# A recommendation model on one core: rows and dense inputs from dumped halves, and two of the first layer's three parts as split float32r passes

## The reference

```
emb = tables[field, sparse]                       # (2048, 26, 32)
linear = lin_sparse_w[field, sparse].sum(-1) + dense @ lin_dense_w
for (w, b) in ((conv1_w, conv1_b), (conv2_w, conv2_b)):     # x0 = xk = emb
    hp = einsum('bhd,bmd->bhmd', xk, x0)          # all products of rows
    xn = sigmoid(w @ hp + b)                      # 128 rows x 32
    xk, rest = xn[:, :64], xn[:, 64:];  keep rest
cin  = concat(rests).sum(-1) @ cin_w + cin_b
deep = tanh chain 845 -> 1024 -> 512 -> 256 on [emb, dense], then @ deep_w + deep_b
out  = linear + cin + deep + bias
```

## Time and profile before

| | before |
|---|---|
| runs, us | 1644.03, 1645.74, 1645.41 (median 1645.41) |
| profiled execution, us | 1642.12, its span 1640.3 |
| PE busy | 1566.3 us, 95% |
| DVE busy | 1143.2 us, 70% |
| ACT busy | 704.7 us, 43% |
| POOL busy | 763.8 us, 47% |
| DMA | 277.60 MB, mean 169 GB/s |
| granted TensorE clock, mean | 0.995 |
| the 64 steps | about 66 to 1354 us |
| the deep layers | 1362 to 1630 us |

### The profile page before, as it was taken

One profiled execution on the slowest core, in us unless ns is written; L12 is line 12 of the kernel. 1 busy time (PEld: TensorE's weight loads), 2 busy tenths in 40 slices (PEclk: granted clock), 3 DMA queues, 4 the chain that ended last, 5 costly groups with the idle time before them and its releaser, 6 DMA issues.

```text
span 1640.3 us, 23407 instructions
## 1 busy us (share of the span) xinstructions
PE 1566.3 (95%) x6840; PEld 681.2 (42%) x6840; DVE 1143.2 (70%) x992; ACT 704.7 (43%) x981; POOL 763.8 (47%) x631
## 2 busy tenths in 40 slices
PE   0599999999999999999999999999999997999998
PEld 0233333333333333333333333333333336787876
DVE  3287878787878787878787878787878783434432
ACT  1344444343444444444344444343444424444543
POOL 7657474757474656565655655664742010000000
PEclk9999999999999999999999999999999999999999
DMA  4688787888887888888888888888888762232231
GB/s 93 124 195 199 189 198 192 194 193 191 196 194 194 194 194 190 193 188 193 195 194 194 194 191 192 193 195 193 196 194 193 185 150 92 92 101 86 89 107 39
DMA packets 111803, 277.60 MB, mean 169 GB/s; under 512 B 26036, under 2 KB 46804, under 8 KB 111704
## 3 DMA queue, kind: packets, MB, share of 16 engines
q1 hardware_dynamic: 98456, 270.11, 66.0%
q0 software_dynamic: 13312, 7.06, 5.3%
HBM read 270.03 MB, written 7.04 MB: 169 GB/s over the span
## 4 chain that ended last, share of the span: by engine, by line
PE 94%; POOL 2%; DVE 1%; ACT 1%; issue 1%; DMA 0%; ACTq 0%; DVEq 0%; POOLq 0%
PE y L636 45%; PE xn L630 21%; PE bc L750 16%; PE bc L616 5%; PE bc L623 3%; PE bc L599 2%; POOL emb L443 2%; PE bc L608 1%; DVE xb L554 0%; ACT sq L806 0%; DVE hp L554 0%; DVE x_lo L563 0%; PE xn L767 0%; DMA sum<-sparse 0%; DMA emb<-table,idx_stage 0%
## 5 line engine op out<-in xcount | busy, mean ns | idle before, releaser
L554 DVE TENSOR_TENSOR hp<-bc,xk 128x1024 f32<-128x1024 f32 x384 | 448.9, 1219 | 264.2 <-PE bc L616 264.2
L554 DVE TENSOR_TENSOR xb<-xb,xk 128x1024 f32<-128x1024 f32 x448 | 581.4, 1355 | 22.8 <-ACT xk L811 22.8
L443 POOL DMA_INDIRECT emb<-table,idx_stage x416 | 495.8, 1192 | 145.9 <-issue 130.5
L636 PE MATMUL y<-xb,w2s 128*64 128x512 f32 x1792 | 423.6, 599 | 0.3 <-ACT r L816 0.3
L636 PE MATMUL y<-hp,w2s 128*64 128x512 f32 x1536 | 368.2, 600 | 0.0
L630 PE MATMUL xn<-sq,w1s 128*128 128x512 f32 x768 | 363.0, 609 | 5.4 <-ACT sq L806 3.2
L806 ACT ACTIVATE sq<-bc 128x1024 f32<-128x1024 f32 x192 | 182.9, 1027 | 261.3 <-PE bc L623 261.3
L810 ACT ACTIVATE xk<-xn,bias 64x512 f32<-64x512 f32 x128 | 87.3, 682 | 376.4 <-PE xn L630 376.4
L458 POOL TENSOR_TENSOR r<-r 128x512 f32<-128x512 f32 x96 | 148.7, 1549 | 144.1 <-ACT r L816 98.4
L630 PEld LDWEIGHTS xn<-sq,w1s 128*128 128x128 f32 x768 | 136.6, 191 | 183.3 <-issue 157.1
L636 PEld LDWEIGHTS y<-xb,w2s 128*64 128x64 f32 x1792 | 117.2, 136 | 214.6 <-issue 188.3
(11 more groups left out here) (63 smaller groups left out, 1056.4 us busy)
## 6 DMA issues: line engine op xcount, KB each, us to landing
xb<-x_rows SPq DMA_DIRECT2D x896, 256.0 KB, 4.9
w_raw<-W SPq DMA_DIRECT2D x32, 448.0 KB, 3.3
w_raw<-W SPq DMA_DIRECT2D x16, 512.0 KB, 3.3
emb<-table,idx_stage POOLq DMA_INDIRECT x416
x_rows<-deep_t SPq DMA_DIRECT2D x16, 384.0 KB
w_raw<-W SPq DMA_DIRECT2D x8, 256.0 KB, 2.7
hp<-select SPq DMA_DIRECT2D x2, 512.0 KB, 4.8
x_rows<-deep_t SPq DMA_DIRECT2D x16, 45.0 KB
```

The costliest lines, as they stand in the source:

```text
L443: nc.gpsimd.indirect_dma_start(out=emb[:, m, :], out_offset=None, in_=table, in_offset=bass.IndirectOffsetOnAxis(ap=idx_stage[:, m:m + 1], ...
L554: nc.vector.tensor_tensor(product(n)[:, :], x[:, :], xk[sl % 2][:, :], ALU.mult).then_inc(multiplied, 1)
L636: last = nc.tensor.matmul(y2[H * c:H * c + H, :], w2s[:, ORDER[n], :], src[:, c * CHUNK:(c + 1) * CHUNK], start=(n == 0), stop=(n == PAIRS ...
```

## The change

- `turn_x0`, `make_high` and `make_low` go. ScalarE's `turned_deep` copies each of now three D fills twice, to `deep_t` (one tile now) and rounded to `deep_halves`; VectorE's `lower_deep` makes the rest; SP dumps both halves to `x0_halves` in HBM and loads `x0t` from there (`load_rows`, four DMAs a step). The D fills stand in step 1 and ahead of fills 3 and 4.
- Of the first layer's three parts, two (k < SPLIT = 2) are made as float32r passes: ScalarE squares them twice (float32 and rounded), GpSimd makes the rest of part 0 and VectorE that of part 1 (`lower_squares` on either engine), and `contract_k` makes three float32r matmuls for each; the third part stays float32. A step's rests are made ahead of contract_k(0) of the same step, which waits for them (`sq_lowered`).
- The deep layers' x is loaded from `x0_halves` and, for the dense inputs, from `dense_halves`, both split before; `upper_x` and `lower_x` go. Weights 0 and 1 are loaded at the start.
- BY_PE is 3, 4, 6, 7, 9, 10 instead of 3, 4, 7, 8, 9, 10; fills and contractions have another order; product 10 shares its buffer with product 3. A spread pair is three DMAs (64, 32 and 32 partitions) instead of two, of the same bytes. GpSimd's order changes. `r1` and `r2` keep a running total in slot 3. Some of the output's terms are moved into the last step, and the four output rows are one instruction.

```
-ORDER = [3, 10, 4, 0, 7, 11, 5, 1, 8, 2, 9, 12, 6]
-BY_PE = (3, 4, 7, 8, 9, 10)
+PER_GROUP = 16
+
+
+ORDER = [0, 1, 2, 3, 8, 4, 5, 9, 6, 7, 10, 11, 12]
+BY_PE = (3, 4, 6, 7, 9, 10)
 assert sorted(ORDER) == list(range(PAIRS))
 BY_DMA = tuple(n for n in range(PAIRS) if n not in BY_PE)
 
 
 
 
-
 STEP_WORK = (
     ("fill", (("K", 0), ("K", 1), ("K", 2))),
-    ("of_last", (9, 10, 11, 12)),
-    ("fill", (("T", 0), ("D", 0), ("D", 1))),
+    ("of_last", (6, 7, 8, 9, 10, 11, 12)),
+    ("fill", (("D", 0), ("D", 1), ("D", 2))),
+    ("fill", (3, 4)),
     ("first", 0),
-    ("fill", (3, 4)),
-    ("of_this", (0, 1, 2)),
+    ("fill", (6, 7)),
+    ("of_this", (0, 1, 2, 3)),
+    ("fill", (9, 10)),
     ("first", 1),
-    ("fill", (7, 8)),
-    ("of_this", (3, 4)),
-    ("fill", (9, 10)),
-    ("of_this", (5, 6, 7, 8)),
+    ("of_this", (4, 5)),
 )
 LEFT = STEP_WORK[1][1]
-SL_DEEP = 2
-DEEP_PARTS = range(0, 4), range(4, KD)
+SL_DEEP = 1
+DEEP_PARTS = range(0, 3), range(3, 5), range(5, KD)
 SLOTS = 3
+R_SLOT = 0, 1, 2, 1
...
+            def dump_halves(t):
+                sp.wait_ge(deep_lowered, t * 2 + 2)
+                hold()
+                for i in range(2):
+                    sp.dma_start(x0_halves[bass.ds(t, 1), i, 0:(KD - 1) * P, :].rearrange("t (k p) b -> p (t k) b", p=P),
+                                 deep_halves[:, i, 0:KD - 1, :].bitcast(F32)).then_inc(halves_dumped, 16)
+                    sp.dma_start(x0_halves[bass.ds(t, 1), i, (KD - 1) * P:M * ROW, :].rearrange("t p b -> p (t b)"),
+                                 deep_halves[0:LAST_E, i, KD - 1, :].bitcast(F32)).then_inc(halves_dumped, 16)
+
+            def await_halves(t):
+                sp.wait_ge(halves_dumped, t * (32 * DUMPS) + 32 * DUMPS)
+                hold()
+
+
+            def load_rows(t, sl):
+                for half in range(2):
+                    rows = x0_halves[bass.ds(t, 1), half, :, :].rearrange("t (m e) b -> (t m) e b", e=ROW)
+                    for c in range(2):
+                        first = sl * STEP_D + c * Q
+                        start = H * c + half
+                        sp.dma_start(x0t[sl][start:start + 2 * M:2, :].bitcast(F32),
+                                     rows[:, first:first + Q, :].rearrange("m d b -> m (d b)")).then_inc(x0_loaded[sl % 2], 16)
+
+
+            def load_x(g, part, parts):
+                loads = []
+                for i, x in enumerate((x_hi, x_lo)):
+                    for k in range(KD):
+                        rows = P if k < KD - 1 else LAST_E
+                        src = x0_halves[bass.ds(g * (CHUNK // P), CHUNK // P), i, k * P:k * P + rows, :]
+                        loads.append((x[0:rows, k, :].bitcast(F32).rearrange("p (t b) -> p t b", b=P),
+                                      src.rearrange("t p b -> p t b")))
+                    loads.append((x[LAST_E:LAST_K, KD - 1, :].bitcast(F32), dense_halves[i, :, bass.ds(g * CHUNK, CHUNK)]))
+                for dst, src in loads[part * X_LOADS // parts:(part + 1) * X_LOADS // parts]:
+                    sp.dma_start(dst, src).then_inc(x_loaded, 16)
...
+                for f, parts in PAIR_ROWS:
                     first = (2 * ORDER[BY_DMA[i]] + f) * ROW + sl * STEP_D
                     row = x0_rows[bass.ds(t, 1), first:first + STEP_D, :].rearrange("t d b -> t (d b)")
-                    sp.dma_start(xb[i][H * f:H * f + H, :], row.to_broadcast([H, COLS])).then_inc(spread[i], 16)
+                    sp.dma_start(xb[i][parts, :], row.to_broadcast([parts.stop - parts.start, COLS])).then_inc(spread[i], 16)
...
+                        if i == 2 and sl == SL_DEEP + 1 and ahead > 0:
+                            dump_halves(t + 1)
+                        if i == 3 and sl == SL_DEEP + 1 and ahead > 0:
+                            await_halves(t + 1)
+                        if i == 3 and (sl < 2 or ahead > 0):
+                            if is_first and sl == 0:
+                                sp.wait_ge(filled, PRO_FILLS)
+                            load_rows(t + (sl + 2) // STEPS, (sl + 2) % STEPS)
+                    if sl == SL_DEEP and ahead > 0:
+                        dump(t + 1)
+                    if sl == 2 and ahead == 0:
+                        sp.wait_ge(dense_dumped, 64)
+                        load_x(0, 0, 1)
...
+            def lower_squares(s):
+                pool.wait_ge(squared, squared_by(s, 0))
+                nc.gpsimd.tensor_tensor(sq_lo[0][:, :], sq[0][:, :], sq_hi[0][:, :], ALU.subtract).then_inc(sq_lowered[0], 1)
...
+            lower_squares(-1)
+            free_emb(0, DEEP_N)
             gather(range(AHEAD[2]))
 
             def tile(t, is_first, ahead):
+                s = t * STEPS
+                lower_squares(s)
+                if ahead > 0:
+                    gather(range(AHEAD[2], M))
                 if not is_first:
                     add_up(t - 1, STEPS - 1, r2, r2_step, y2_read, 1, sum2)
+                lower_squares(s + 1)
+                add_up(t, 1, r1, r1_step, xn_read, 2, sum1)
+                if ahead > 1:
+                    free_emb(t + 1, filled_by(t, SL_DEEP, ("D", DEEP_N - 1), ahead))
+                    gather(range(AHEAD[0]))
+                lower_squares(s + 2)
+                add_up(t, 2, r1, r1_step, xn_read, 2, sum1)
+                if ahead > 1:
+                    gather(range(AHEAD[0], AHEAD[1]))
+                add_up(t, 1, r2, r2_step, y2_read, 1, sum2)
                 if ahead > 0:
-                    gather(range(AHEAD[2], M))
-                add_up(t, 1, r1, r1_step, xn_read, 2, sum1)
-                if ahead > 0:
-                    make_low(t + 1)
-                add_up(t, 2, r1, r1_step, xn_read, 2, sum1)
-                add_up(t, 1, r2, r2_step, y2_read, 1, sum2)
-                if ahead > 1:
-                    free_emb(t + 1, filled_by(t, SL_DEEP, ("D", 1), ahead))
-                    gather(range(AHEAD[0]))
+                    lower_squares(s + 3)
                 add_up(t, 3, r1, r1_step, xn_read, 2, sum1)
                 if ahead > 1:
-                    gather(range(AHEAD[0], AHEAD[1]))
+                    gather(range(AHEAD[1], AHEAD[2]))
                 add_up(t, 2, r2, r2_step, y2_read, 1, sum2)
-                if ahead > 1:
-                    gather(range(AHEAD[1], AHEAD[2]))
 
...
+            def lower_deep(t):
+                dve.wait_ge(deep_rounded, t * DEEP_N + DEEP_N)
+                for rows, ks in ((slice(0, P), slice(0, KD - 1)), (slice(0, LAST_E), slice(KD - 1, KD))):
+                    nc.vector.tensor_tensor(deep_halves[rows, 1, ks, :], deep_t[rows, ks, :],
+                                            deep_halves[rows, 0, ks, :], ALU.subtract).then_inc(deep_lowered, 1)
...
+            def lower_squares(s):
+                dve.wait_ge(squared, squared_by(s, 1))
+                nc.vector.tensor_tensor(sq_lo[1][:, :], sq[1][:, :], sq_hi[1][:, :], ALU.subtract).then_inc(sq_lowered[1], 1)
...
+                        if n == 2 and not (ahead == 0 and sl == STEPS - 1):
+                            lower_squares(s)
                         if n in BY_PE:
                             dve.wait_ge(filled, filled_by(t, sl, n, ahead))
-                            if not start:
-                                dve.wait_ge(contracted, contracted_by(s - 1, n))
+                            if n == BY_PE[-1]:
+                                dve.wait_ge(contracted, contracted_by(s, BY_PE[0]))
+                            elif not start:
+                                dve.wait_ge(contracted, contracted_by(s - 1, BY_PE[-1] if n == BY_PE[0] else n))
                             x = bc[slot_of(sl, n, ahead)]
                         else:
                             i = BY_DMA.index(n)
-                            dve.wait_ge(spread[i], s * 32 + 32)
+                            dve.wait_ge(spread[i], s * (16 * len(PAIR_ROWS)) + 16 * len(PAIR_ROWS))
                             x = xb[i]
                         nc.vector.tensor_tensor(product(n)[:, :], x[:, :], xk[sl % 2][:, :], ALU.mult).then_inc(multiplied, 1)
-                        if n == 8 and sl == 1 and ahead > 0:
+                        if n == 3 and sl == SL_DEEP and ahead > 0:
                             sum_linear(t + 1)
+                        if n == 7 and sl == SL_DEEP and ahead > 0:
+                            dve.wait_ge(halves_dumped, t * (32 * DUMPS) + 32 * DUMPS)
+                            lower_deep(t + 1)
...
-                for k in range(K1):
-                    last = nc.tensor.matmul(xn[:, :], w1s[:, k, :], sq[k][:, cols], start=(k == 0), stop=(k == K1 - 1))
+                for k in range(SPLIT):
+                    for i, (w, x) in enumerate(((w1_hi, sq_hi[k][:, cols]), (w1_lo, sq_hi[k][:, cols]),
+                                                (w1_hi, sq_lo[k][:, cols]))):
+                        nc.tensor.matmul(xn[:, :], w[:, k, :], x, start=(k == 0 and i == 0), stop=False)
```

(33 more changed lines are left out.)

354 lines of the change are left out of this document (171 added, 183 removed).

## The result

| | before | after |
|---|---|---|
| median, us | 1645.58 | 1703.41 (1699.85 to 1708.88, four runs) |
| ratio, 95% interval | | 1.0356 [1.0327, 1.0386] |
| profiled execution, its span, us | 1642.12, 1640.3 | 1699.85, 1698.0 |
| granted TensorE clock, mean | 0.995 | 0.98 |

The kernel is slower by 3.6%. The sign, the engine and the place were forecast, the size was not: the median rose by 57.8, where +32 had been put. It lies at the very end of the range, 1704 (1703.4 as a median; the ratio 1.0356 times 1645.6 is 1704.2). The forecast itself was 25 too low.

What follows compares the result with a forecast made beforehand. VectorE, blocked by GpSimd through the shared port pair, was taken to bound the changed kernel: tiles +19, start +20.6, end -7.7, together +32 us, giving 1678 as a median, range 1632 to 1704.

Steps and rivals of the forecast that it cites:

- TensorE's part: TensorE in the tile loop: ordinary steps fall from 19.94 to 18.6 us, its floor for a tile is 77.1.
- ScalarE's doubled copies: Step with the deep rows: fills 3 and 4 wait for ScalarE's two copies, some 1.9 us of TensorE wait.
- The saving of the float32r passes alone: First layer on TensorE: six float32r matmuls replace two float32 ones, saving 0.4 us twice a step, 0.8.
- The mechanism: Tile loop: GpSimd's rest locks the port pair shared with VectorE, costing its SBUF products the whole 2.41 us a step.
- B: Rival, faster: TensorE stays the bound at contract_k(0), tiles of 78 us, total 1619 (1605 to 1640); chance 0.19.
- D: Rival, slower: GpSimd's rest takes 3.1 us, tiles of 84.5, +60 + 13, total 1718; chance 0.08.
- the sum of a tile: VectorE's work plus its losses to GpSimd: 81.8 us a tile against today's 80.56, +19 over 15.25 tiles.
- rival C: Slower: the DMA engines bound through added dumped and loaded bytes, perhaps 83.5 us a tile, total 1703; chance 0.10.
- The start: Step 0's rest waits behind 20 gathers in GpSimd's queue; step 1's fill at 109 instead of 88.2, +20.6 us.
- Rival E: The start doesn't stall because the first rest is in time: 20 us less than the forecast, 1657; chance 0.05.
- The end: Last tile-loop steps up to the deep layers: 43.4 us plus one of wait instead of 45.8, -3 without slow matmuls.
- The output's part: After ScalarE's last deep activation: only wdo (about 2.0 us) and one activation of 0.69 remain, -4.7.

Runs made afterwards that it cites:

- g1: f3 with the deep layers' x loads put behind the last step's spreads: 1617.9 us, ratio 0.984.
- g3: The changed kernel with all three first-layer parts in float32 again (no rests) and row loads issued by ScalarE: 1645.2 us, ratio 1.0001.
- g2: The changed kernel with only the row loads issued by ScalarE instead of SyncE, GpSimd keeping its rest: 1688.2 us.
- f3: e2 with the row loads issued by ScalarE and SyncE no longer waiting in the step for the halves' dump: 1624.4 us, ratio 0.9884.
- e1: The changed kernel with GpSimd's rest in the steps cut from 1024 columns to one: 1692.4 us.
- e2: The changed kernel with both rests made by VectorE and none by GpSimd: 1688.9 us.
- f4: The changed kernel with all three first-layer parts in float32 again, without rests or rounded copies: 1690.2 us.
- e4: The changed kernel with six instead of 20 gathers ahead of step 0's rest at the start, the others behind it: 1710.0 us.
- e3: The changed kernel with a spread pair as two DMAs instead of three, 18 instead of 25 issues a step: 1702.1 us.

## Why the prediction was right and where it was wrong

**TensorE's part was right.** The floor was put at 77.1 with steps of 18.6. In g1 undisturbed steps take 18.7 and the one with the deep rows 20.9: 77.0 for four (its mean tile is 78.4, with small waits left). ScalarE's doubled copies (0.49, 0.38 forecast) stall it 1.24 once a tile, 18.7 in all, where I had put 1.9. The saving of the float32r passes alone, g3's step against g1's, is 0.65, forecast 0.8.

**The mechanism was right, its size a little high.** GpSimd's rest takes 2.36 alone (2.41 forecast) and costs VectorE 2.2. TensorE's waits for the rests in the steps are 55.3 + 3.9 = 59.2, 3.9 a tile, where my sum had VectorE 4.7 above TensorE's floor. g2 confirms it without SyncE: 43.2 + 7.0, 3.3 a tile. Against f3 the GpSimd rest costs 64.7 of span, 3.5 a tile and 11.4 at the start. Rivals B (TensorE bound) and D (rest of 3.1) are out.

**The step that failed is the sum of a tile.** It read "81.8, above TensorE's 77.1", and two terms were missing from it. They make 12 of the 25 us by which the forecast fell short; 9 are the last step's (below), 4 the deep layers'. First the clock: waits of 2 us in step 2 are often followed by a stretch at 1.2 GHz, 1.3 us lost a tile (1.1 in g2). I had given such a price to the start, and none to the repeated waits that I had myself forecast as "1 to 2 us in three of four steps". Second SyncE: I counted bytes on the DMA engines (rival C) and cost 11 more issues a step at nothing. With 0.65 us each for spreads, 0.96 for row loads, the dumps between them and the pause at the loop's end, SyncE needs some 82 a tile. In the change as it stands this adds only 0.8 (82.6 against g2's 81.8), 12 us in 15.25 tiles, since VectorE is nearly as late anyway; in the versions without GpSimd's rest that keep three DMAs a pair and the row loads on SyncE (e1, e2, f4) it is the bound. The clock's 1.3 and SyncE's 0.8 stand against waits that were 0.8 smaller than forecast or partly the same time; I can't divide the 82.6 into exact shares.

**The start was right:** 108.87 against 109, by its mechanism (11.91 us of wait behind GpSimd's rest, which ended at 96.1, forecast 96; the idle stretch forecast as some 19 us is broken by a fill at 83.50). e4 adds that the order of the gathers can't mend it. Rival E is out.

**The end was wrong in one term.** "The x loads have the 27 us of layers two and three: nothing" looked at bytes and at a later group. The first group's 16 loads stand in SyncE's queue ahead of the last step's spreads, and the stretch took 52.8 instead of 43.4. g1 moves them, takes 44.7 for it and ends 7 us earlier than f3. The output's part (-4.5) came as forecast.

**Open:** the deep layers' matmuls begin 0.232 us apart (61.32 for 264) instead of 0.228, worth most of the +3.2; in g1, 62.78 for 264 with a slow start of some 1.4. The change touches neither, the DMA engines are busier beside it (152 against 98 GB/s over 1440 to 1500), but no run tells a cause. Nor was a run made that keeps the 2 us waits and avoids the lower clock: its 1.3 a tile is read from rows, not tested alone. And what of SyncE's 82 matters most (the number of issues, the wait for the dumps in its queue, the pause at the loop's end) is open, since every run that took the row loads from SyncE took the wait with them.

## What to carry to other kernels

Count DMAs issued per step on each queue, not only bytes: at 0.65 to 0.96 us each SyncE is an engine with a budget like the others, and an idle engine's queue may take some of them. Look also for a wait that stands in a queue ahead of issues which don't need it, and for a pause at the end of a loop whose code has grown. When one bound is removed and nothing moves, suspect a second at the same height and fill in the corners of the table; here two single fixes brought 10 to 12 us each and both together 75. A wait of about 2 us on TensorE that recurs may cost as much again in the clock behind it.

## What the runs showed of the hardware

- SyncE takes 0.65 us per spread DMA of 32 or 64 partitions in a row (21 in 13.73), 0.96 per row load of 26 partitions (4 in 3.82), with nothing waited for; the 0.65 was the same at a DMA share of 0.70 and of 0.95. Where ScalarE issued such row loads (f3), TensorE waited for loaded rows ten times in the steps, 9.1 us in all.
- SyncE paused 3.1 to 3.7 us at each of the 12 turns of the tile loop, with five instruction loads of 8 KB a turn; with seven DMAs fewer a step (e3) it paused 0.24 to 0.27, with no such loads in the loop after its first turn.
- A GpSimd subtraction and the add right behind it both ran at full length (2.36 and 1.27), while VectorE's subtraction, recorded as begun first, took 5.03. VectorE's products from PSUM kept their 1.21 in the mean.
- Behind waits of 1.96 us or more the clock fell to 1.2 GHz, mostly for some 3.4 us, eleven times in this kernel's steps; in f3, g1 and g3, which have the 1.24 us waits of every tile too, it fell nowhere in the steps. The length of one wait doesn't decide it: in e1 it fell six times behind waits of 0.77 to 1.62 us (five of them with another of some 0.6 close by), and in e3 eleven waits of 1.94 to 2.06 us had nothing behind them.
- The same bytes spread as two halves of the partitions instead of a middle and two quarters raised the DMA engines' share from 0.81 to 0.91 at 209 to 210 GB/s.
